# Two-pass attention and int8 FFN layer on 8 cores: order of the score and value products, placement of the normalised tile, and engine of the q/k bias add

## The reference

```python
x = L0_attn_x                                   # (16, 2048, 1024) f32
h = layernorm(x)
q, k, v = split(h @ Wqkv + bqkv, 3)             # D = 1024
attn = (q @ k.T) / sqrt(1024)
attn = attn * mask        # gamma**(i-j), 0 for i<j, in the same 128-block; 1 elsewhere
attn = softmax(attn)
x = x + (attn @ v) @ Wproj + bproj
h = layernorm(x)
gate = h @ (w_gate / 127).T ; up = h @ (w_up / 127).T     # hidden 3072
x = x + (silu(gate) * up) @ (w_down / 127).T
```

## Time and profile before

| what | us |
|---|---|
| median of 3 runs | 6683.36 |
| lowest and highest of them | 6080.63, 7056.36 |
| profiled execution | 6119.29 |
| its span on the slowest core (core 3) | 6117.7 |
| spans of the 8 cores | 6045.8 to 6117.7 |

### The profile page before, as it was taken

How to read it: one execution, slowest core, us unless ns; L and a number is a source line. 1 busy time by engine, 2 the same in 40 slices (tenths; PEclk the granted TensorE clock), 3 DMA queues, 4 the chain that set the end, 5 groups by cost and what they waited for, 6 DMA issues and landing times.

```text
span 6117.7 us, 54596 instructions; the slowest of 8 cores (6045.8 to 6117.7 us)
## 1 busy us (share of the span) xinstructions
PE 5068.6 (83%) x22794; PEld 2332.9 (38%) x22794; DVE 1123.2 (18%) x1409; ACT 617.6 (10%) x928; POOL 65.3 (1%) x94
## 2 busy tenths in 40 slices
PE   0898888892887788857788888798989989898989
PEld 0333333340333333323333333344444444444444
DVE  2222222220111111101111111211111212111111
ACT  2000000000001000000000000111110101011110
POOL 1100000000000000000000000000000000000000
PEclk9879999995998899979899999899999999999999
DMA  6611111115001000030100000421211212121211
GB/s 129 79 40 55 55 55 55 55 43 184 14 21 29 23 21 21 21 120 22 31 21 21 21 21 21 94 79 49 66 59 59 66 49 85 43 80 45 69 56 42
DMA packets 253337, 324.43 MB, mean 53 GB/s; under 512 B 129188, under 2 KB 161956, under 8 KB 252070
## 3 DMA queue, kind: packets, MB, share of 16 engines
q1 hardware_dynamic: 144214, 201.38, 10.9%
q0 software_dynamic: 61776, 52.43, 4.4%
q10 hardware_dynamic: 47104, 67.12, 3.1%
HBM read 255.87 MB, written 96.47 MB: 58 GB/s over the span
## 4 chain that ended last, share of the span: by engine, by line
PE 79%; DMA 10%; DVE 5%; issue 3%; ACT 2%; SPq 0%; DVEq 0%; ACTq 0%; POOLq 0%
PE ps L210 37%; PE ps L564 12%; PE ps L650 11%; PE ps L911 11%; PE ps L703 6%; DMA qt_hi<-q_scr 3%; DMA qt_lo<-q_scr 1%; DMA wtmp<-wqkv 1%; PE ps L805 1%; PE ps L367 1%; DVE ao L663 1%; DVE x1t L710 1%; DVE x1t L714 1%; DMA wptmp<-wproj 1%; DMA q_scr<-qf_lo 1%
## 5 line engine op out<-in xcount | busy, mean ns | idle before, releaser
L564 PE MATMUL ps<-k_hi,qt_hi 128*128 128x512 bf16 x1024 | 298.0, 462 | 351.3 <-DMA qt_lo<-q_scr 178.2
L210 PE MATMUL ps<-xn2f_hi,wgbuf 128*128 128x512 bf16 x1536 | 376.3, 389 | 22.4 <-DVE xn2f_lo L823 22.4
L210 PE MATMUL ps<-xn2f_lo,wgbuf 128*128 128x512 bf16 x1536 | 370.5, 385 | 0.0
L210 PE MATMUL ps<-xn2f_hi,wubuf 128*128 128x512 bf16 x1536 | 362.8, 379 | 0.0
L210 PE MATMUL ps<-xn2f_lo,wubuf 128*128 128x512 bf16 x1536 | 362.8, 379 | 0.0
L911 PE MATMUL ps<-wd_sb,hf_hi 128*128 128x512 bf16 x1536 | 336.7, 379 | 20.8 <-DVE hf_lo L886 20.8
L911 PE MATMUL ps<-wd_sb,hf_lo 128*128 128x512 bf16 x1536 | 336.7, 379 | 0.0
L564 PEld LDWEIGHTS ps<-k_hi,qt_hi 128*128 128x128 bf16 x1024 | 114.9, 114 | 531.2 <-issue 458.7
L879 DVE SCALAR_TENSOR_TENSOR h<-ps,sgb 128x512 f32<-128x512 f32 x192 | 132.8, 691 | 949.7 <-PE ps L210 949.7
L210 PE MATMUL ps<-xnf_hi,wq_hi 128*128 128x512 bf16 x1024 | 272.7, 415 | 2.6 <-DVE xnf_lo L381 2.6
L367 PE MATMUL ps<-ident,xnA 128*128 128x128 f32 x256 | 45.7, 338 | 271.3 <-DVE xnA L358 271.3
(11 more groups left out here) (112 smaller groups left out, 4240.6 us busy)
## 6 DMA issues: line engine op xcount, KB each, us to landing
wgbuf<-wg_scr SPq DMA_DIRECT2D x192, 256.0 KB, 2.6
wubuf<-wu_scr SPq DMA_DIRECT2D x192, 256.0 KB, 2.9
xsA<-x SPq DMA_DIRECT2D x32, 512.0 KB, 3.6
xres<-x SPq DMA_DIRECT2D x32, 512.0 KB, 4.6
x_scr<-x1t POOLq DMA_DIRECT2D x32, 512.0 KB, 6.1
x1A<-x_scr SPq DMA_DIRECT2D x32, 512.0 KB, 3.4
y<-outA ACTq DMA_DIRECT2D x32, 512.0 KB, 2.7
wtmp<-wqkv SPq DMA_DIRECT2D x8, 1536.0 KB, 7.6
```

The source lines that it names most:

```text
L210: e.matmul(psum_ap, l, r, start=st, stop=sp),
L564: kb=kb, st=first, sp=last: e.matmul(ps0[:, kb * 512:kb * 512 + KW], lhs, kx[:, dc * S + kb * KW: dc * S + (kb + 1) * KW], start=st, stop=sp),
```

## The change

Five edits:

1. `emit_xn_tr` is cut in two. `emit_xn`, which writes `xnA` on VectorE, is now emitted after the first of every four q/k groups, and the transposes and copies still after the fourth.
2. The first of the two PSUM reads of a q/k group (`qf_hi`, `kf_hi`) goes from VectorE (L416) to ScalarE as an add of the bias (L417 after the change).
3. In stage B the scores of `g + 1` and the prefetch of its q tile are emitted behind the values of `g` for every tile, not only at a sequence's last.
4. The softmax of `g + 1` is emitted behind the copies of the output transposes of `g`, ahead of the projection of `g`. So its `exp` now waits for the last read of `ao32`.
5. `ell` and `invl` have one column instead of two, and two waits go with that.

```diff
+        def emit_xn(st, j):
             t_xn[(st, j)] = P("vector", ... xnA ...)
+
+        def emit_xn_tr(st, j):
...
-                th = P("vector", lambda e, bank=bank, dsth=dsth, cc=cc,
-                       bias=bias: e.tensor_scalar(
-                           dsth[:, cc * TA:(cc + 1) * TA], bank, bias, None,
-                           OP.add),
+                th = P("scalar", lambda e, bank=bank, dsth=dsth, cc=cc,
+                       bias=bias: e.add(
+                           dsth[:, cc * TA:(cc + 1) * TA], bank, bias),
                        waits=[tmm, t_bq, t_store["q" if ec < 8 else "k"]],
-                       inc="ve")
+                       inc="sc")
...
+                if ec % 4 == 0 and st + 1 < NST:
+                    emit_xn(st + 1, ec // 4)
                 if ec % 4 == 3 and st + 1 < NST:
                     emit_xn_tr(st + 1, ec // 4)
...
-            seq_boundary = (g + 1) % NQT == 0
-            if g + 1 < NG and not seq_boundary:
-                prefetch_q(g + 1)
-                emit_scores(g + 1)
-                emit_softmax(g + 1)
...
-            if g + 1 < NG and seq_boundary:
+            if g + 1 < NG:
                 prefetch_q(g + 1)
-                emit_kv(s + 1, [t_scmm[g], lastav])
+                if (g + 1) % NQT == 0:
+                    emit_kv(s + 1, [t_scmm[g], lastav])
                 emit_scores(g + 1)
-                emit_softmax(g + 1)
...
             t_aofl[g] = t_aof_ev[1]
+            if g + 1 < NG:
+                emit_softmax(g + 1)
             lastpj = None
```

More of the change, by code:

```diff
@@ L118, in build_program @@
         mx_b = sb("mx_b", [128, 2], F32)
-        ell = sb("ell", [128, 2], F32)
-        invl = sb("invl", [128, 2], F32)
+        ell = sb("ell", [128, 1], F32)
+        invl = sb("invl", [128, 1], F32)
         rem = nc.sbuf_bytes_remaining
@@ L353, in emit_loads_stats @@
             t_chain[st] = t_c6
-        def emit_xn_tr(st, j):
-            par = st % 2
-            xb = par * DC * TA
+        def emit_xn(st, j):
             t_xn[(st, j)] = P("vector", lambda e, j=j: e.tensor_scalar(
@@ L362, in emit_xn_tr @@
                 waits=[t_chain[st], tr_prev[0]], inc="ve")
-            if (st, j - 1) not in t_ev and j == 0:
-                pass
+        def emit_xn_tr(st, j):
+            par = st % 2
+            xb = par * DC * TA
             tr = None
@@ L390, in build_program @@
         for j in range(NSUB):
+            emit_xn(0, j)
             emit_xn_tr(0, j)
@@ L583, in emit_softmax @@
                 waits=[t_mx], inc="ve")
-            pl_ = g % 2
-            te_ = P("scalar", lambda e, pl_=pl_: e.activation(
+            te_ = P("scalar", lambda e: e.activation(
                 a32[:, 0:S], ps0[:, 0:S], AF.Exp, bias=mx_b[:, 1:2],
-                scale=isqd, accum_out=ell[:, pl_:pl_ + 1]),
+                scale=isqd, accum_out=ell[:, 0:1]),
                 waits=[t_ng, t_lastArt.get(g - 1), t_aoev.get(g - 1),
-                       t_aofl.get(g - 1), t_il.get(g - 2)],
+                       t_aofl.get(g - 1)],
                 inc="sc")
             t_exp[g] = te_
-            t_il[g] = P("vector", lambda e, pl_=pl_: e.reciprocal(
-                invl[:, pl_:pl_ + 1], ell[:, pl_:pl_ + 1]),
-                waits=[te_, t_aoev.get(g - 2)], inc="ve")
+            t_il[g] = P("vector", lambda e: e.reciprocal(
+                invl[:, 0:1], ell[:, 0:1]), waits=[te_], inc="ve")
         t_il = {}
@@ L657, in build_program @@
             t_avmm[g] = lastav
-            if g + 1 < NG and seq_boundary:
+            if g + 1 < NG:
                 prefetch_q(g + 1)
-                emit_kv(s + 1, [t_scmm[g], lastav])
+                if (g + 1) % NQT == 0:
+                    emit_kv(s + 1, [t_scmm[g], lastav])
                 emit_scores(g + 1)
-                emit_softmax(g + 1)
-            t_ao = P("vector", lambda e, pg=g % 2: e.scalar_tensor_tensor(
-                ao32[:, :], ps1[:, :], invl[:, pg:pg + 1], bv_b[:, :],
+            t_ao = P("vector", lambda e: e.scalar_tensor_tensor(
+                ao32[:, :], ps1[:, :], invl[:, 0:1], bv_b[:, :],
                 OP.mult, OP.add),
```

## The result

| | before | changed |
|---|---|---|
| profiled execution, us | 6119.3 | 5755.8 |
| lowest of all runs, us | 6078.6 | 5750.8 |
| median of all runs, us | 6731.0 (10) | 5825.3 (8) |
| ratio of the times | 1 | 0.9459 [0.944, 0.9477] |

They put before at 6080 and the changed kernel at 5753 us, 327 less. The forecast was 5850, a gain of 269, in a range of 5755 to 5985.

The account below looks back on a forecast made before the run. TensorE was taken to bound the kernel, so only its idle time could be gained: 6119.3 less 99 in stage A and 170 in stage B gives 5850 us, in a range of 5755 to 5985.

Parts of the forecast that it names:

- The base: Whole program: all sums were made against the profiled execution of the kernel before, 6119.3 us.
- Stage A, 99 us: Stage A: earlier `xnA` and the bias add on ScalarE save 59.2, 30 and 10 us; bounds 88 and 112.
- the short waits: Stage A, TensorE waiting for `xnA`: 22 waits of 2.69 us each go whole, 59.2 us.
- the six long ones: Stage A, `xnA` waits at the first quarter of 6 steps: 5.0 us less each, 30 us; about 7.5 us stay.
- Stage B, 170 us: Stage B: 29 tiles 5.63 us shorter, 7.7 at the sequence's end, about 1 lost at tile 0; bounds 89 and 251.
- the slow start at the values: Stage B: first 32 matmuls of the values take 9.70 us instead of 6.91, 2.79 us a tile.
- the hidden softmax: Stage B: next tile's softmax, 5.37 us, runs beside the projection, 10.53 us, with 5 us of slack.
- the q load's slack: Stage B: the q load has 28 us to land, where both halves took 9.4, so scores do not wait.
- warmer start: Stage B: with fewer pauses the values start at full speed, stage B gives 251 us, 5769 in all; chance 0.09.
- Exchange only: Stage B: the pause moves from scores to values and eats the q wait's gain; 6012 us; chance 0.06.
- the disturbed ScalarE: Stage A: bias adds wait behind stores on ScalarE, four groups fill `ps0`, 96 us come; 5946 us; chance 0.05.
- The slower side: Whole program: TensorE's clock falls below its upper level, 6215 or up to 6940 us; clock case 0.10, slower 0.03.

Follow-up runs that it names:

- the two runs of the parts: Kernel before with only stage A's edits (1 and 2): lowest 5975.1 us; kernel before with only stage B's edits (3 to 5): lowest 5856.7 us.
- copies-first: Changed kernel with VectorE's projection bias add, residual add and row sum put behind `at_lo` copies of the attention transposes: 6106.5 us, run again 5641.1 us.
- q-first run: Kernel before with only the next q tile's load moved ahead of the residual rows on SyncE: lowest 5894.5 us, ratio 0.9688.

## Why the prediction was wrong

The direction and the mechanism stood, the time did not: 5753, 97 us below the forecast. By its own steps:

- **The base.** All sums were made against 6119.3 us. Its slowest core had a stretch at a lower clock that six of the eight cores had not. The stretch of the earlier trace rows at 0.81 on core 3 reads on core 4 of the same execution, and on the changed kernel's core 1:

```profile
163.00:540.00 377.00, 328.98 (x1504) 152.08 (x1503) 109.55 (x148) 32.75 (x51) 21.71 (x26) 0.95 0.34 67
```

```profile
163.00:540.00 377.00, 354.91 (x1660) 166.39 (x1659) 86.01 (x115) 68.22 (x104) 21.71 (x26) 0.97 0.38 74
```

  1504 matmuls instead of 1312 in the time of the earlier trace rows. The forecast saw the 0.81 and used it for a rival, but left it in the base, as if the change would keep it. Without it, before is at 6080: 39 us.

- **Stage A, 99 us.** Measured 100, and its parts as worked out: the short waits gone, five of the six long ones 5 to 6 us shorter. The first of the six took 13.85 us on core 1 of the changed kernel, as long as before. Right all the same. That the bias add matters so little beside edit 1 fits too.

- **Stage B, 170 us: mis-sized.** Measured 223. This is the step that failed, and in it first the slow start at the values. The step read: "9.70 us for the first 32 matmuls where later ones take 6.91", from tile 15, and said that this tile "had the same neighbours before them as all will have". In the changed kernel these 32 take 8.82 us at the tile shown, and 8.2 to 9.1 at any tile of cores 1 and 5, tile 15 among them: a slow start of 1.9 us instead of 2.79. One row was too little to see how far the size can move. In the same execution of the kernel before, the chains of core 4 and of core 7 have for tile 15:

```profile
2578.21 22.46 PE ps L650 x96
```

```profile
2576.18 23.75 PE ps L650 x96
```

  Core 5 is like core 4 (8.5 to 8.6 us for the first 32), the other six have 9.4 to 9.8. The mean of the eight is about 9.4, so more rows would have mended only a third of the term. The neighbours were not the same either: before tile 15 the projection of tile 14 comes after a wait for `ao` of 1.54 us, and in the changed kernel the output transposes and that projection follow 96 dense matmuls without it. Whether this shortens the slow start was not tried; its cause stays open.

  The sum of the gap: projection to values took 18.68 us instead of 18.94, the slow start was 0.89 shorter, and 0.04 lies in the rest, together 1.19 us a tile or 35 us in 29 tiles. The length of the tile before gave 13: the ten tiles from 1897 to 2614 took 71.67 each, but all 29 took 72.1 on core 4 (72.0 on core 3), as the steady stretch leaves out the tiles with slower projections. The last tile and its projection gave 3 more, for which nothing had been set, and the sequence's end and tile 0 about 1 each. That is the 53. From its first matmul to its last, stage B is 2363 us on core 4 before and 2141 on core 1 after.

- **Stage C and the rest** moved by no more than 4 us; what was forecast for the hidden softmax, the q load's slack and `ao` came out as written.

39 + 1 + 53 and 4 us, by which the two runs of the parts (323) fall short of the whole (327), make the 97. Of the rivals, "warmer start" was closest, in time (5769) and in kind, but that it comes so near is luck: it had the values start at full speed and stage B give 251 us. They do start slowly, only less so, stage B gave 223, and the 39 us of the base made up the rest. "Exchange only" and the disturbed ScalarE within stage A did not occur, though ScalarE's stores do hold its adds, at the first group of each step. The slower side, a clock below its upper level, came and went in both kernels alike.

The Trainium skill's rule that the forecast weighed ("TensorE: Matmul & The Clock Gate", "Part 1: The HAM clock gate") holds the clock down while three cores of a die run dense matmuls. The stretch at 0.79 in the first copies-first run agrees with it; the execution of the same program in which all eight cores had a mean clock of 0.95 does not. The measurement decides: dense work on all cores can go with the lowered clock but does not bring it each time.

## What to carry to other kernels

When a load stands in a queue behind one that waits for late work, move the load before reordering the compute: one moved line gave 186 of 223 us here. Where two instructions of one engine serve TensorE and a later consumer, put those for TensorE first; that was worth another 112 us. Before adding up waits against a profiled time, compare the granted clock of the same stretch on all cores. Read a size that carries a term, such as a slow start, from all tiles and cores, and if it was read behind other work than the change will put before it, give it a range and not a value.

## What the runs showed of the hardware

- The lowered clock comes and goes with the same instructions. The copies-first kernel ran at 6106.5 us with all cores near a mean clock of 0.873, and at 5641.1 with all at 0.951. Nor does it take the same stretch of the program on all cores of a die: in the first of these, core 1 had 0.81 between 163 and 540 us and 0.96 between 4500 and 5300, core 3 had 0.97 and 0.79.
- The slow start after a break in the large matmuls is a lower granted clock (0.77 from 2118.5 to 2127 us in the changed kernel), and it hardly depends on the length of the pauses in the break. With pauses of 3.99 and 1.62 us and transposes around them the first 32 matmuls took 8.82 us, with 1.18 and 1.70 they took 8.59 at most tiles. But at tile 16 of core 0, behind the same two pauses, they took 6.90, at a granted clock of 1.00:

```profile
2436.43 1.22 PE L616 MATMUL ps<-ident,a 128*128 128x128 f32 x8 [1.18 <-DVE at_lo L625]
2439.35 7.07 PE L651 MATMUL ps<-v_hi,at_hi 128*128 128x512 bf16 x32 [1.70 <-DVE at_lo L625]
2446.25 4.05 PE L651 MATMUL ps<-v_lo,at_hi 128*128 128x512 bf16 x18
```

  So the pauses alone do not set it. Where there is only one pause, of 4.34 us, and the matmuls follow the transposes directly (the q-first run), they took 7.6 to 8.6 us, and the projection had its own slow start. Why was not tried.
- A bias add of 128x512 from PSUM on ScalarE takes 0.6 us back to back (2.40 for four), nearly a plain copy's 586 ns; the same on VectorE takes 0.75.
